# A graph network's update pass with VectorE's sum and shift in the other order, and the root of two norms taken over degree times variance

## The chip, the cores and the metric

One Trainium2 chip (trn2), one of its cores. The kernel is one program with one launch. The metric is the device time of one execution in microseconds (us), taken as the median of repeated runs. TensorE multiplies, VectorE and ScalarE do the elementwise work, GpSimd issues indirect DMAs, and SyncE and ScalarE issue the plain ones.

## The reference, cut to what matters

Four graph layers run over x (10000 nodes by 768 features, fp32), each followed by a layer norm without learned parameters. The parts that the change touches, in the reference's words:

```
x = _layernorm(x + L0(x))          # combined = concat([x, out2]); combined @ Wu + bu     -> update pass
x = _layernorm(x + L1(x))          # relu(heads' residual + attention sum)                -> heads pass
x = _layernorm(x + L2(x))          # graph convolution, norm = dinv[src] * dinv[dst]      -> conv layer "cv"
x = _layernorm(x + L3(x))          # two graph convolutions                               -> "c3a", "c3b"

def _layernorm(x, axis=-1, eps=1e-05):
    m = jnp.mean(x, axis=axis, keepdims=True)
    v = jnp.var(x, axis=axis, keepdims=True)
    return (x - m) / jnp.sqrt(v + eps)
```

A convolution weighs a source row by dinv[src] = 1/sqrt(deg[src]), where deg is the number of edges that end in the node, its own loop among them. The kernel puts that factor into the table that the convolution reads: the heads pass and layer cv write their normed rows times dinv, so the number that they store is (y - m) / sqrt(v + eps) * dinv.

## The kernel before, in words

The 10000 rows are worked in 79 tiles of 128 rows (the last has 16). A stage is a block in which every engine has its own instruction stream over the 79 tiles, written by `over_tiles`: the first four steps are written out, then a loop of four steps a turn, then the last three tiles and the steps that drain the pipeline. The order in each stream is fixed by its `step` function; the engines meet only at semaphores. `back(t, slot, turn, k)` names the tile k steps before the current one; `slot` is the tile's number modulo 4 and `s2` its number modulo 2.

The stages in order of time: first_layers (to about 1276 us of the span), the update pass (`update_pass`, 1280 to 1585 us), the third layer's attention, the heads pass (`heads_pass`, about 1750 to 2095 us), and the conv layers cv, c3a and c3b (`conv_layer`, from about 2100 us to the end).

The update pass, tile t:

- SyncE loads 96 KB of out2 into o2[slot] and 396 KB of u into ut[slot], each once a slot of four is free (for u: once the sum of tile t-4 is made).
- TensorE turns o2 over (`turn_over`, two transposes, in step t), and one step later multiplies it with w_up into one of two PSUM buffers, `prods` (`multiply`, four fp32 products that the trace shows as eight matmul records). The product of tile t waits until the sum of tile t-2 has read its buffer.
- VectorE's `end(t)`: the sum y = prods + ut (L1496), two halves of statistics (L1499, L1500), a memset and their aggregate (L1503), which gives mean and variance in mv.
- ScalarE's `root_of(t)`: root = sqrt(variance + eps) (L1540).
- VectorE's `shift_of(t)`: rstd = 1/root (L1508), shift = -mean*rstd (L1510), and three small pieces of the 25 extra columns (L1511, L1514, L1517). It waits for the root, and for the store of tile t-4, whose x_o buffer it writes.
- ScalarE's `polish(t)`: x_o = y*rstd + shift (L1548), then `store` one step later: 396.5 KB to x1 (L1554) and 12.5 KB to sc3 (L1555).

VectorE's step s runs `shift_of(s-3)` and then `end(s-2)`. ScalarE's step s runs `turn_back(s)` (PSUM to ot, L1535), `root_of(s-2)`, `polish(s-3)` and the store of s-4. `y` has two buffers, so `end(t)` waits until tile t-2 has been polished.

The heads pass and cv end in the same way with their own tiles (hds_, cv_). There `shift_of` has three VectorE instructions: rstd = 1/root (L2148, L2423), rstd = rstd * dinv (L2150, L2426), shift (L2152, L2428). The heads pass also has VectorE's `add` (hds_x, L2128) ahead of these, which TensorE's second six transposes of a tile wait for. In c3b (the last layer) rstd is not multiplied, and c3a has no norm.

Of the kernel before, what the change touches and what calls it, by code (L numbers as in the profile page):

```python
# [8 lines left out]
I32 = mybir.dt.int32  # L9
# [3 lines left out]
P = 128  # L13
N = 10000
E = 12500
D = 768
# [119 lines left out]
def build(nc, a, out):  # L136
# [15 lines left out]
    with ExitStack() as ctx:  # L152
        def sb(name, shape, dt=F32):
# [11 lines left out]
            "one_i": sb("one_i", [P, NT], I32), "sq": sb("sq", [P, NT]),  # L165
# [47 lines left out]
def first_layers(nc, g, a, packed, packed2, sources, agg, h1, sc1, h2, out2, u, x2, x3):  # L213
# [3 lines left out]
    with ExitStack() as ctx:  # L217
# [417 lines left out]
        def _(dve):  # L635
# [137 lines left out]
            bg.to(AT_NODE + 1)  # L773
            dve.wait_ge(deg_root, 1)
# [662 lines left out]
def update_pass(nc, g, u, out2, x1, sc3):  # L1437


    with ExitStack() as ctx:  # L1440
# [6 lines left out]
        y = sb("y", [P, 2, CU])  # L1447
# [39 lines left out]
        def _(dve):  # L1487
            v = nc.vector

            def end(t, slot, turn):  # L1490
                s2 = slot % 2
                dve.wait_ge(u_in[slot], turn * 16 + 16)
                dve.wait_ge(multiplied, t + 1)
                if at_least(t, 2):
                    dve.wait_ge(polished, t - 1)
                v.tensor_tensor(y[:, s2, :].rearrange("p (a f) -> p a f", a=2), prods[s2][:, :, 0:HALFC],  # L1496
                                ut[:, slot, :].rearrange("p (a f) -> p a f", a=2), ALU.add).then_inc(prod_read, 1)
                dve.wait_ge(prod_read, t + 1)
                v.bn_stats(stats[:, s2, 0, :], y[:, s2, 0:HALF]).then_inc(halved, 1)  # L1499
                v.bn_stats(stats[:, s2, 1, :], y[:, s2, HALF:D]).then_inc(halved, 1)  # L1500
                dve.wait_ge(halved, t * 2 + 2)
                v.memset(scrap[:, :], 0.0)
                v.bn_aggr(mv[:, s2, :], stats[:, s2, :, :].rearrange("p a s -> p (a s)")).then_inc(spread, 1)  # L1503

            def shift_of(t, slot, turn):
                s2 = slot % 2
                dve.wait_ge(rooted, t + 1)
                v.reciprocal(rstd[:, s2, :], root[:, s2, :]).then_inc(shifted, 1)  # L1508
                dve.wait_ge(shifted, t * 2 + 1)
                v.scalar_tensor_tensor(shift[:, s2, :], mv[:, s2, 0:1], -1.0, rstd[:, s2, :], ALU.mult, ALU.mult).then_inc(shifted, 1)  # L1510
                v.tensor_scalar(part[:, s2, :], y[:, s2, D:CU], rstd[:, s2, :], None, ALU.mult).then_inc(parted, 1)  # L1511
# [18 lines left out]
        def _(act):  # L1530
# [11 lines left out]
            def polish(t, slot, turn):  # L1542
# [5 lines left out]
                nc.scalar.activation(x_o[:, slot, 0:D], y[:, s2, 0:D], ACT.Identity, bias=shift[:, s2, :],  # L1548
# [482 lines left out]
def heads_pass(nc, g, a, x1, agg, x2):  # L2031
# [4 lines left out]
    with ExitStack() as ctx:  # L2036
# [78 lines left out]
        def _(dve):  # L2115
# [29 lines left out]
            def shift_of(t, slot, turn):  # L2145
# [25 lines left out]
        def _(act):  # L2171
# [6 lines left out]
            def root_of(t, slot, turn):  # L2178
                act.wait_ge(spread, t + 1)
                nc.scalar.activation(root[:, slot % 2, :], mv[:, slot % 2, 1:2], ACT.Sqrt, bias=g["eps"][:, 0:1]).then_inc(rooted, 1)  # L2180

            def polish(t, slot, turn):
                s2 = slot % 2
                act.wait_ge(shifted, t * 3 + 3)
# [60 lines left out]
def conv_layer(nc, g, tag, table, out, weights, bias, res=None, first=False, last=False):  # L2245
# [4 lines left out]
    with ExitStack() as ctx:  # L2250
# [6 lines left out]
        K = 2 if last else 3  # L2257
# [103 lines left out]
        def _(dve):  # L2361
# [58 lines left out]
            def shift_of(t, slot, turn):  # L2420
# [3 lines left out]
                if not last:  # L2424
                    dve.wait_ge(shifted, t * K + 1)
                    v.tensor_scalar(rstd[:, s2, :], rstd[:, s2, :], g["dinv"][:, bass.ds(t, 1)], None, ALU.mult).then_inc(shifted, 1)  # L2426
                dve.wait_ge(shifted, t * K + (K - 1))
# [16 lines left out]
        def _(act):  # L2444
# [32 lines left out]
            def root_of(t, slot, turn):  # L2477
                act.wait_ge(spread, t + 1)
                nc.scalar.activation(root[:, slot % 2, :], mv[:, slot % 2, 1:2], ACT.Sqrt, bias=g["eps"][:, 0:1]).then_inc(rooted, 1)

            def polish(t, slot, turn):
                s2 = slot % 2
                if norm:
                    act.wait_ge(shifted, t * K + K)
# [112 lines left out]
```

## Time and profile before

| What | Value |
|---|---|
| Median of 3 runs | 3884.01 us (3877.66 to 3886.38) |
| The profiled execution's own time | 3883.69 us |
| Its span in the trace | 3881.9 us, 64638 instructions |
| Granted TensorE clock, mean | 0.966 of full |
| TensorE busy, whole span | 3556.3 us (92%) |
| VectorE busy | 2481.6 us (64%) |
| ScalarE busy | 1366.8 us (35%) |
| Update pass, 1300 to 1575 us | TensorE 232.6, VectorE 222.3, ScalarE 120.9 of 275 us |

The page is one execution as the profiler saw it. Busy time is the union of an engine's instructions. The time outside the span is 3883.69 - 3881.9 = 1.8 us. An average over the span says little of one stage, so the stages have to be read one by one: by windows, by the table of waits, and by the timeline of a single tile.

### The profile page before, as it was taken

Reading aid. Unit: us, or ns where it says so; the run is one execution under the profiler, and the core shown is the slowest. Engines: PE = TensorE matmul, PEld = TensorE weight load, DVE = VectorE, ACT = ScalarE, POOL = GpSimd, SP = SyncE. Lnnn points to the kernel's source line nnn. Section 1 sums busy time; section 2 is a strip of 40 time slices with the busy share of each in tenths; the row PEclk is TensorE's granted clock in tenths of the full one; section 3 lists DMA queues with packets and bytes.
Section 4 is the critical chain, followed back from the end, with each engine's and each line's share of the span. In section 5 each row is a group of like instructions: output and inputs, shape, how many; then the busy total and the mean of one; then the engine's idle time right before and its main releaser. Section 6 shows DMA issues by size and latency. Waiting matters only on the chain. (4 is left out here: it accounts for less than half of the span.)

```text
span 3881.9 us, 64638 instructions
## 1 busy us (share of the span) xinstructions
PE 3556.3 (92%) x21125; PEld 3356.1 (86%) x21125; DVE 2481.6 (64%) x4955; ACT 1366.8 (35%) x1888; POOL 1092.4 (28%) x1533
## 2 busy tenths in 40 slices
PE   7999999999999888258996999998899998899999
PEld 6999999999999544138995999997899998799999
DVE  4877986158433588347996777776344443577777
ACT  2222232222222344115664344443333332344443
POOL 5540200414512100427774222221222221322221
PEclk9999999999999999679998999999999999999999
DMA  4777887658754688425665333334333333455554
GB/s 113 238 235 212 238 250 242 190 184 268 225 180 142 198 251 253 139 75 173 212 212 177 104 127 126 126 127 144 108 126 125 127 128 117 157 183 186 184 184 142
DMA packets 363376, 672.37 MB, mean 173 GB/s; under 512 B 100181, under 2 KB 193010, under 8 KB 363242
## 3 DMA queue, kind: packets, MB, share of 16 engines
q1 hardware_dynamic: 248154, 441.01, 37.3%
q10 hardware_dynamic: 70160, 155.79, 10.3%
q0 software_dynamic: 44928, 73.84, 6.8%
q8 instruction: 78, 1.28, 0.1%
q14 instruction: 56, 0.46, 0.0%
HBM read 429.79 MB, written 346.94 MB: 200 GB/s over the span
## 5 line engine op out<-in xcount | busy, mean ns | idle before, releaser
L716 DVE TENSOR_TENSOR fr_lo<-fr_turned_ps,fr_hi 128x768 fp32r<-128x768 f32 x158 | 150.4, 952 | 240.0 <-ACT fr_hi L1140 240.0
L1592 PE MATMUL up_prod<-w_up,up_ot 128*128 128x396 f32 x632 | 231.4, 510 | 40.9 <-DVE up_y L1496 40.9
L2408 DVE SCALAR_TENSOR_TENSOR c3a_y<-c3a_prod,dinv,next_const 128x768 f32<-128x768 f32 x79 | 80.4, 1018 | 288.8 <-PE c3a_prod L2564 288.8
L1284 PE MATMUL fr_prod<-fr_w_hi,fr_hi 128*128 128x396 f32 x948 | 257.1, 352 | 0.0
L1284 PE MATMUL fr_prod<-fr_wu_hi,fr_hi 128*128 128x396 f32 x948 | 254.7, 349 | 0.0
L1284 PE MATMUL fr_prod<-fr_w_lo,fr_hi 128*128 128x396 f32 x948 | 249.3, 344 | 0.0
L2564 PE MATMUL cv_prod<-next_w_hi,cv_hi 128*128 128x384 f32 x948 | 248.9, 344 | 0.0
L2564 PE MATMUL c3a_prod<-next_w_hi,c3a_hi 128*128 128x384 f32 x948 | 248.9, 344 | 0.0
L1284 PE MATMUL fr_prod<-fr_w_hi,fr_lo 128*128 128x396 f32 x948 | 248.7, 343 | 0.0
L2564 PE MATMUL c3b_prod<-next_w_hi,c3b_hi 128*128 128x384 f32 x948 | 248.6, 344 | 0.0
L1284 PE MATMUL fr_prod<-fr_wu_lo,fr_hi 128*128 128x396 f32 x948 | 248.3, 343 | 0.0
L1284 PE MATMUL fr_prod<-fr_wu_hi,fr_lo 128*128 128x396 f32 x948 | 247.8, 342 | 0.0
L2564 PE MATMUL cv_prod<-next_w_hi,cv_lo 128*128 128x384 f32 x948 | 241.8, 336 | 0.0
L2564 PE MATMUL c3a_prod<-next_w_hi,c3a_lo 128*128 128x384 f32 x948 | 241.8, 336 | 0.0
L2564 PE MATMUL cv_prod<-next_w_lo,cv_hi 128*128 128x384 f32 x948 | 241.7, 336 | 0.0
L2564 PE MATMUL c3b_prod<-next_w_lo,c3b_hi 128*128 128x384 f32 x948 | 241.7, 336 | 0.0
L2564 PE MATMUL c3a_prod<-next_w_lo,c3a_hi 128*128 128x384 f32 x948 | 241.6, 336 | 0.0
L2564 PE MATMUL c3b_prod<-next_w_hi,c3b_lo 128*128 128x384 f32 x948 | 241.6, 336 | 0.0
L1140 ACT ACTIVATE fr_hi<-fr_turned_ps 128x768 fp32r<-128x768 f32 x158 | 127.2, 805 | 322.1 <-PE fr_turned_ps L1268 322.0
L1592 PEld LDWEIGHTS up_prod<-w_up,up_ot 128*128 128x128 f32 x632 | 114.7, 191 | 126.0 <-ACT up_ot L1535 44.8
L2475 ACT ACTIVATE c3a_hi<-c3a_turned_ps 128x768 fp32r<-128x768 f32 x79 | 64.1, 812 | 356.2 <-PE c3a_turned_ps L2553 356.2
L2232 PE MATMUL hds_prod<-hds_w_st,hds_hi 128*128 128x128 f32 x948 | 184.3, 276 | 0.0
(588 smaller groups left out, 9109.0 us busy)
## 6 DMA issues: line engine op xcount, KB each, us to landing
fr_ins<-in_x_dram SPq DMA_DIRECT2D x156, 384.0 KB, 4.2
x<-fr_zrow SPq DMA_DIRECT2D x156, 384.0 KB
x<-up_x_o ACTq DMA_DIRECT2D x78, 396.5 KB, 3.5
h<-fr_outs SPq DMA_DIRECT2D x78, 396.0 KB
u<-fr_outs SPq DMA_DIRECT2D x78, 396.0 KB
up_ut<-u SPq DMA_DIRECT2D x78, 396.0 KB
agg<-fr_zrow SPq DMA_DIRECT2D x78, 390.0 KB
hds_row<-x SPq DMA_DIRECT2D x78, 384.0 KB, 3.2
```

The costliest lines, as they stand in the source:

```text
L716: v.tensor_tensor(lo[:, s2, :, :], turned_ps[:, 0:KC, :], hi[:, s2, :, :].bitcast(F32), ALU.subtract).then_inc(split_done, 1)
L1140: nc.scalar.activation(hi[:, t % 2, :, :], turned_ps[:, 0:KC, :], ACT.Copy).then_inc(hi_done, 1)
L1284: made = nc.tensor.matmul(prods[s2][:, bank, 0:c1 - c0], l[:, s2, s, :], w[:, s, c0:c1], start=(s == 0 and i == 0), stop=(s == KC - 1 and ...
L1592: made = nc.tensor.matmul(prods[s2][:, half, 0:HALFC], ot[:, s2, k, :], g["w_up"][:, k, half * HALFC:(half + 1) * HALFC], start=(k == 0), ...
L2232: nc.tensor.matmul(o, hi[:, s2, s, :], w_st[:, 0, :], start=True, stop=False)
L2408: v.scalar_tensor_tensor(y3, p3, g["dinv"][:, bass.ds(t, 1)], c3, ALU.mult, ALU.add).then_inc(prod_read, 1)
L2475: nc.scalar.activation(hi[:, slot % 2, :, :], turned_ps[:, 0:KC, :], ACT.Copy).then_inc(hi_done, 1)
L2564: made = nc.tensor.matmul(prods[s2][:, a, 0:HALF], l[:, s2, s, :], w[:, s, a * HALF:(a + 1) * HALF], start=(s == 0 and i == 0), stop=(s == ...
```

## The change

Three edits.

1. In the update pass, VectorE's step s runs `end(s-2)` first and `shift_of(s-3)` behind it. `y` has four buffers (indexed by slot, not by s2). The wait for the polish moves: `end(t)` no longer waits for `polished`; `shift_of(t)` waits until tile t-1 has been polished.
2. In the heads pass and in cv, the VectorE instruction rstd = rstd*dinv goes. In its place the root is taken of deg*variance + deg*eps: ScalarE's activation reads a column of `deg` as its scale and a column of `deg_eps` as its bias. 1/sqrt(deg*(v + eps)) is the same number as dinv/sqrt(v + eps). c3b keeps its root.
3. In first_layers two VectorE instructions make the two arrays, each 128x79.

The diff, cut to its core:

```
@@ first_layers, after the node lists
+            link(v.tensor_copy(g["deg"][:, :], pt["deg"][:, :]))
+            link(v.tensor_scalar(g["deg_eps"][:, :], pt["deg"][:, :], EPS, None, ALU.mult))
@@ update_pass
-        y = sb("y", [P, 2, CU])
+        y = sb("y", [P, UNROLL, CU])
@@ end(t)
                 dve.wait_ge(multiplied, t + 1)
-                if at_least(t, 2):
-                    dve.wait_ge(polished, t - 1)
-                v.tensor_tensor(y[:, s2, :]..., prods[s2][:, :, 0:HALFC],
+                v.tensor_tensor(y[:, slot, :]..., prods[s2][:, :, 0:HALFC],
...
@@ shift_of(t)
                 dve.wait_ge(rooted, t + 1)
+                if at_least(t, 1):
+                    dve.wait_ge(polished, t)
                 v.reciprocal(rstd[:, s2, :], root[:, s2, :]).then_inc(shifted, 1)
...
@@ step(t)
+                b = back(t, slot, turn, 2)
+                if at_least(t, 2) and live(b[0]):
+                    end(*b)
                 b = back(t, slot, turn, 3)
                 if at_least(t, 3) and live(b[0]):
                     shift_of(*b)
-                b = back(t, slot, turn, 2)
-                if at_least(t, 2) and live(b[0]):
-                    end(*b)
@@ heads_pass and conv_layer (there unless it is the last): shift_of
                 v.reciprocal(rstd[:, s2, :], root[:, s2, :]).then_inc(shifted, 1)
-                dve.wait_ge(shifted, t * 3 + 1)
-                v.tensor_scalar(rstd[:, s2, :], rstd[:, s2, :], g["dinv"][:, bass.ds(t, 1)], None, ALU.mult).then_inc(shifted, 1)
-                dve.wait_ge(shifted, t * 3 + 2)
+                dve.wait_ge(shifted, t * 2 + 1)
@@ root_of
-                nc.scalar.activation(root[...], mv[...], ACT.Sqrt, bias=g["eps"][:, 0:1])
+                nc.scalar.activation(root[...], mv[...], ACT.Sqrt, bias=g["deg_eps"][:, bass.ds(t, 1)],
+                                     scale=g["deg"][:, bass.ds(t, 1)])
```

VectorE's stream at the start of the update pass, before (up_y is the sum, up_mv the aggregate, up_rstd to the second up_x_o the five instructions of the shift; a row is an instruction, with its line, output and inputs):

```order
L1496 TENSOR_TENSOR up_y<-up_prod,up_ut 128x792
L1499 BN_STATS up_stats<-up_y 128x6
L1500 BN_STATS up_stats<-up_y 128x6
L1502 MEMSET up_scrap 128x1
L1503 BN_AGGR up_mv<-up_stats 128x2
L1508 RECIPROCAL up_rstd<-up_root 128x1
L1510 SCALAR_TENSOR_TENSOR up_shift<-up_mv,up_rstd 128x1
L1511 TENSOR_SCALAR up_part<-up_y,up_rstd 128x24
L1514 COPY up_x_o<-own 128x1
L1517 SCALAR_TENSOR_TENSOR up_x_o<-v_sum,up_shift,up_part 128x24
L1496 TENSOR_TENSOR up_y<-up_prod,up_ut 128x792
```

The same place in the changed kernel, from the aggregate of tile 0 on:

```order
L1503 BN_AGGR up_mv<-up_stats 128x2
L1496 TENSOR_TENSOR up_y<-up_prod,up_ut 128x792
L1499 BN_STATS up_stats<-up_y 128x6
L1500 BN_STATS up_stats<-up_y 128x6
L1502 MEMSET up_scrap 128x1
L1503 BN_AGGR up_mv<-up_stats 128x2
L1510 RECIPROCAL up_rstd<-up_root 128x1
L1512 SCALAR_TENSOR_TENSOR up_shift<-up_mv,up_rstd 128x1
L1513 TENSOR_SCALAR up_part<-up_y,up_rstd 128x24
L1516 COPY up_x_o<-own 128x1
L1519 SCALAR_TENSOR_TENSOR up_x_o<-v_sum,up_shift,up_part 128x24
```

The shift of tile 0 stood directly behind the aggregate of tile 0; now the whole sum and statistics of tile 1 stand between them, and so on for every tile: five instructions of a tile's shift are passed by the five of the next tile's sum.

VectorE's stream in one step of the heads pass, before (hds_y is the sum, hds_own_w and hds_x belong to a later tile):

```order
L2122 SCALAR_TENSOR_TENSOR hds_own_w<-hds_more,has_in,has_own 128x12
L2148 RECIPROCAL hds_rstd<-hds_root 128x1
L2150 TENSOR_SCALAR hds_rstd<-hds_rstd,dinv 128x1
L2152 SCALAR_TENSOR_TENSOR hds_shift<-hds_mv,hds_rstd 128x1
L2136 SCALAR_TENSOR_TENSOR hds_y<-hds_prod,hds_row 128x768
```

And in the changed kernel:

```order
L2124 SCALAR_TENSOR_TENSOR hds_own_w<-hds_more,has_in,has_own 128x12
L2150 RECIPROCAL hds_rstd<-hds_root 128x1
L2152 SCALAR_TENSOR_TENSOR hds_shift<-hds_mv,hds_rstd 128x1
L2138 SCALAR_TENSOR_TENSOR hds_y<-hds_prod,hds_row 128x768
```

One instruction has gone between the reciprocal and the shift; nothing else moved. In cv it is the same.

## Rows read from the trace of the kernel before

**Rows 1.** By stretch: length; busy of PE, PEld, DVE, ACT, POOL; clock; DMA share; GB/s.
```profile
1300.00:1575.00 275.00, 232.59 (x744) 127.51 (x742) 222.28 (x750) 120.88 (x224) 0.00 (x0) 1.00 0.83 246
1800.00:2050.00 250.00, 244.13 (x2187) 241.79 (x2186) 228.57 (x608) 161.87 (x183) 198.19 (x243) 1.00 0.65 213
2145.00:2690.00 545.00, 543.20 (x3301) 540.21 (x3299) 426.39 (x859) 226.88 (x307) 102.76 (x220) 1.00 0.36 120
```

**Rows 2.** Waits, update pass: who waited for whom, us, times, longest.
```profile
ACT up_root L1540 <- DVE up_mv L1503: 138.8, 75, 2.2
...
PE up_prod L1592 <- DVE up_y L1496: 40.5, 74, 0.8
DVE up_rstd L1508 <- ACT up_root L1540: 27.2, 75, 0.4
...
DVE up_y L1496 <- ACT up_x_o L1548: 13.6, 58, 0.4
```

**Rows 3.** Timeline, VectorE: start, duration (us), instruction, idle before and its releaser.
```profile
1422.46 0.98 DVE L1496 TENSOR_TENSOR up_y<-up_prod,up_ut 128x792 f32<-128x792 f32 x1 [0.21 <-ACT up_x_o L1548]
...
1424.54 0.20 DVE L1503 BATCH_NORM_AGGREGATE up_mv<-up_stats 128x2 f32<-128x12 f32 x1
...
1425.11 0.16 DVE L1508 RECIPROCAL up_rstd<-up_root 128x1 f32<-128x1 f32 x1 [0.36 <-ACT up_root L1540]
...
1425.65 0.24 DVE L1517 SCALAR_TENSOR_TENSOR up_x_o<-v_sum,up_shift,up_part 128x24 f32<-128x24 f32 x1
1426.09 0.98 DVE L1496 TENSOR_TENSOR up_y<-up_prod,up_ut 128x792 f32<-128x792 f32 x1 [0.20 <-ACT up_x_o L1548]
```

**Rows 4.** The same stretch on ScalarE.
```profile
1424.78 0.29 ACT L1540 ACTIVATE up_root<-up_mv,eps 128x1 f32<-128x1 f32 x1 [1.90 <-DVE up_mv L1503]
1424.98 1.01 ACT L1548 ACTIVATE up_x_o<-up_y,up_shift,up_rstd 128x768 f32<-128x768 f32 x1
```

**Rows 5.** Timeline, TensorE, the first tiles of the update pass.
```profile
1284.50 5.03 PE L1592 MATMUL up_prod<-w_up,up_ot 128*128 128x396 f32 x8
...
1289.59 2.83 PE L1592 MATMUL up_prod<-w_up,up_ot 128*128 128x396 f32 x8
...
1292.47 2.83 PE L1592 MATMUL up_prod<-w_up,up_ot 128*128 128x396 f32 x8
```

**Rows 6.** Timeline, VectorE, tiles 0 and 1 of the update pass.
```profile
1293.85 0.24 DVE L1517 SCALAR_TENSOR_TENSOR up_x_o<-v_sum,up_shift,up_part 128x24 f32<-128x24 f32 x1
1294.01 0.98 DVE L1496 TENSOR_TENSOR up_y<-up_prod,up_ut 128x792 f32<-128x792 f32 x1
```

**Rows 7.** One tile's view, up_y: times, min/median/max ns, first and last start.
```profile
L1496 DVE TENSOR_TENSOR up_y<-up_prod,up_ut x79: 976/983/983, 1289.6 to 1576.4; 128x792 f32<-128x792 f32 x79
```

**Rows 8.** Timeline, ScalarE, last polish of the update pass.
```profile
1579.90 1.03 ACT L1548 ACTIVATE up_x_o<-up_y,up_shift,up_rstd 128x768 f32<-128x768 f32 x1
```

**Rows 9.** DMA issues, update pass: KB each, median us to landing.
```profile
x<-up_x_o ACTq DMA_DIRECT2D x75, 396.5 KB, 3.5
up_ut<-u SPq DMA_DIRECT2D x71, 396.0 KB
up_o<-out SPq DMA_DIRECT2D x70, 96.0 KB, 3.4
```

**Rows 10.** Busy by stretch, the update pass's busiest 5 us for the DMA.
```profile
1540.00:1545.00 5.00, 4.05 (x15) 2.27 (x14) 4.29 (x13) 1.75 (x4) 0.00 (x0) 1.00 0.94 333
```

**Rows 11.** Timeline, VectorE, one tile of the heads pass.
```profile
1900.83 0.16 DVE L2148 RECIPROCAL hds_rstd<-hds_root 128x1 f32<-128x1 f32 x1
...
1901.37 0.16 DVE L2152 SCALAR_TENSOR_TENSOR hds_shift<-hds_mv,hds_rstd 128x1 f32<-128x1 f32 x1
```

**Rows 12.** Waits of TensorE in the heads pass, steady stretch.
```profile
PE hds_turned_ps L2222 <- DVE hds_x L2128: 5.8, 5, 2.1
```

**Rows 13.** Waits of VectorE in the heads pass.
```profile
DVE hds_x L2128 <- issue: 3.5, 12, 0.3
```

**Rows 14.** One line's view, L771: a VectorE operation on 128x79.
```profile
L771 DVE TENSOR_TENSOR fr_node_f<-fr_node_f,fr_node x1: 241/241/241, 244.3 to 244.3; 128x79 f32<-128x79 f32 x1
```

More of the change, by code:

```diff
@@ L164, in build @@
             "total_i": sb("total_i", [P, 1], I32), "total2_i": sb("total2_i", [P, 1], I32),
-            "one_i": sb("one_i", [P, NT], I32), "sq": sb("sq", [P, NT]),
+            "one_i": sb("one_i", [P, NT], I32), "sq": sb("sq", [P, NT]), "deg": sb("deg", [P, NT]), "deg_eps": sb("deg_eps", [P, NT]),
             "src2_i": sb("src2_i", [P, NC], I32), "put2_i": sb("put2_i", [P, NC], I32),
@@ L1547, in polish @@
                     act.wait_ge(stored[slot], turn * 32)
-                nc.scalar.activation(x_o[:, slot, 0:D], y[:, s2, 0:D], ACT.Identity, bias=shift[:, s2, :],
+                nc.scalar.activation(x_o[:, slot, 0:D], y[:, slot, 0:D], ACT.Identity, bias=shift[:, s2, :],
                                      scale=rstd[:, s2, :]).then_inc(polished, 1)
@@ L2179, in root_of @@
                 act.wait_ge(spread, t + 1)
-                nc.scalar.activation(root[:, slot % 2, :], mv[:, slot % 2, 1:2], ACT.Sqrt, bias=g["eps"][:, 0:1]).then_inc(rooted, 1)
+                nc.scalar.activation(root[:, slot % 2, :], mv[:, slot % 2, 1:2], ACT.Sqrt, bias=g["deg_eps"][:, bass.ds(t, 1)],
+                                     scale=g["deg"][:, bass.ds(t, 1)]).then_inc(rooted, 1)
             def polish(t, slot, turn):
                 s2 = slot % 2
-                act.wait_ge(shifted, t * 3 + 3)
+                act.wait_ge(shifted, t * 2 + 2)
                 if at_least(t, UNROLL):
@@ L2256, in conv_layer @@
         L = 2 if apart else 1
-        K = 2 if last else 3
         rows_in = sb("row", [P, UNROLL, D])
@@ L2423, in shift_of @@
                 v.reciprocal(rstd[:, s2, :], root[:, s2, :]).then_inc(shifted, 1)
[L2424 to L2427, printed above, removed]
+                dve.wait_ge(shifted, t * 2 + 1)
                 v.scalar_tensor_tensor(shift[:, s2, :], mv[:, s2, 0:1], -1.0, rstd[:, s2, :], ALU.mult, ALU.mult).then_inc(shifted, 1)
@@ L2478, in root_of @@
                 act.wait_ge(spread, t + 1)
-                nc.scalar.activation(root[:, slot % 2, :], mv[:, slot % 2, 1:2], ACT.Sqrt, bias=g["eps"][:, 0:1]).then_inc(rooted, 1)
+                if last:
+                    nc.scalar.activation(root[:, slot % 2, :], mv[:, slot % 2, 1:2], ACT.Sqrt, bias=g["eps"][:, 0:1]).then_inc(rooted, 1)
+                else:
+                    nc.scalar.activation(root[:, slot % 2, :], mv[:, slot % 2, 1:2], ACT.Sqrt, bias=g["deg_eps"][:, bass.ds(t, 1)],
+                                         scale=g["deg"][:, bass.ds(t, 1)]).then_inc(rooted, 1)
             def polish(t, slot, turn):
@@ L2483, in polish @@
                 if norm:
-                    act.wait_ge(shifted, t * K + K)
+                    act.wait_ge(shifted, t * 2 + 2)
                 else:
```

8 lines of the change are left out of this document (4 added, 4 removed).

## The prediction

> **What bounds the kernel now.** I read the busy shares first, then windows of the stages that the diff touches, then the waits inside them, and last the timeline of single tiles. The page's total (TensorE 92%, in the table above) says that most stages are TensorE's, and the windows say which. In cv TensorE is busy 543.2 of 545 us; in the heads pass 244.1 of 250; in the update pass only 232.6 of 275, with VectorE at 222.3, ScalarE at 120.9 and the DMA engines at 0.83 of full [rows 1]. So the update pass is the one stage of the three in which no engine is full, and a chain through several of them sets the pace. The reader is to look for that chain.
>
> The waits show it: VectorE waits 75 times for the root (27.2 us) and 58 times for the polish (13.6 us), and TensorE waits 74 times for the sum, 40.5 us; ScalarE waits 138.8 us for the aggregate [rows 2]. One tile in order of time: sum at 1422.46, aggregate from 1424.54 to 1424.74 [rows 3], root at 1424.78, polish of the tile before at 1424.98 to 1425.99 [rows 4], next sum at 1426.09 [rows 3]. Every link waits for the one in front, round a ring of 3.63 us. VectorE's shift (1425.11 to 1425.89) lies inside the polish's time. TensorE is in the ring only as a follower: in the first tiles, where no sum had to be waited for, one multiply began 2.88 us after the other (1289.59, 1292.47), with the transposes between them [rows 5]. The first sum starts at 1289.6 and the last at 1576.4, 78 steps of 3.68 us [rows 7].
>
> **The new period of the update pass.** With the sum first, the sum of tile t+1 no longer needs the polish of t-1, as it has a buffer of its own, and the shift of t comes a whole sum and its statistics after the root of t. Both of VectorE's waits in a period, 0.36 and 0.20 us [rows 3], go. 3.63 - 0.36 - 0.20 = 3.07 us. The same from the parts: sum to aggregate 2.08, reciprocal to the last instruction of the shift 1425.65 - 1425.11 = 0.54 [rows 3], and two joints. The joint from the shift's last instruction to a sum that waits for nothing is 0.16 us, less than that instruction's 0.24 [rows 6]; the joint from the aggregate (0.20) to the reciprocal is not in the trace, and taken with the same overlap of 0.08 it is 0.12. Low end: 2.08 + 0.12 + 0.54 + 0.16 = 2.90. High end, each joint a full duration plus 0.04: 2.08 + 0.24 + 0.54 + 0.28 = 3.14. A VectorE that always has work also pays its loop's turn: in the heads pass 0.3 us of "issue" once in four tiles (3.5 us in 12) [rows 13], 0.07 us a tile. So 2.97 to 3.21, and I take 3.05, close to the 3.07 of the subtraction, which is the nearest row.
>
> The Trainium skill, VectorE: DVE Perf Modes, section "The DRAIN you can't avoid", speaks for the high end: an operation does not start before the pipe of the one in front is empty; it adds that one that is not held back starts earlier. By its first sentence the period would be 3.21, by its second the 2.97. The trace has the overlap at the one joint seen (0.08 us) [rows 6].
>
> What is late next? The other cycles are shorter. TensorE: 2.88 us a tile [rows 5]. ScalarE: 120.9 us in 275/3.65 = 75 tiles is 1.61 us [rows 1]. Polish of t-1 now follows the shift of t-1, which follows the aggregate of t; behind the polish ScalarE copies the turned tile for a later multiply, and that feeds a sum three tiles on: about 2.98 (sum to end of shift) + 0.05 + 1.01 (polish) + 0.6 (rest of ScalarE's tile) + 2.83 (multiply) + 0.1 = 7.6 us for three tiles, 2.5 us each. The moved wait stands in front of the reciprocal, with the whole shift and the next sum queued behind it; but the polish of t-2 that it asks for begins when the shift of t-2 ends, some 2.2 us earlier, and takes 1.01. That leaves 1.1 us of cover; without it VectorE, and with it all others, would wait. The root has a full period of cover. SyncE's loads keep their waits and their order; they are asked for earlier, as each sum is.
>
> Sum for the pass. The product of tile 2 is made by 1292.47 + 2.83 = 1295.3 [rows 5]; sum 1 no longer stands behind shift 0, so sum 2 can start then. Sum 78 starts at 1295.3 + 76 x 3.05 = 1527.1, against 1576.4: -49.3 us. The end gets longer. Before, the last polish started 1579.90 - 1576.4 = 3.5 us after the last sum [rows 7, 8]. Now shift 77 stands behind aggregate 78 and ends at 2.98; polish 77 ends at 4.0; only then may shift 78 run (0.78), and polish 78 starts at 4.9: +1.4 us. Together -47.9.
>
> **The other edits.** In the heads pass the removed instruction lies between a reciprocal and a shift that are 0.54 us apart [rows 11]; the reciprocal takes 0.16 of them, so with the instruction gone VectorE gets back up to 0.35 us a tile. TensorE is at 98% there and waited for VectorE's hds_x only 5 times, 5.8 us in 250 [rows 1, 12]. Ends: nothing, if those waits come from late loads, or all of TensorE's idle time, 5.9/250 over some 330 us, 8 us. I take -3, as the next load of a row waits for this tile's sum, which comes earlier. The root with two columns for scale and bias: ScalarE has time to spare (162 of 250 us busy), so 0.1 us more in it costs nothing; if it were on the path it would be 79 x 0.1 = 8 us, kept for the range. In cv TensorE is full to 0.3%: 0, as its products cover VectorE's 0.2 us; uncovered it would be 79 x 0.25 = 20 us of gain, which 543.2 of 545 excludes [rows 1]. First_layers gets two operations on 128x79, 0.24 us each [rows 14] plus a wait: +0.6 us if nothing covers them, 0 if TensorE does; I take +0.3.
>
> Total: 3883.7 (the profiled execution's own time, 0.3 under the median of the runs) - 47.9 - 3 + 0.3 = 3833; with the 0.3 to the median, 3833.4. I say 3834.
>
> **Rivals.** *The DMA becomes the bound.* A tile moves 396.5 + 396 + 96 KB and 12.5 KB more, 901 KB or 0.923 MB [rows 9]; at 3.05 us that is 303 GB/s. For it: 0.83 of full at 246 GB/s puts the ceiling at 296, a period of 3.11 [rows 1]. Against it: 333 GB/s at 0.94 in one stretch of the same pass [rows 10], a ceiling of 354 and 2.6 us. At 3.11 it would cost 5 us and stay in my range. As a rival of its own I take a rate midway between today's and that ceiling, 271 GB/s: 3.40 us, sum 78 at 1553.7, -22.7 + 1.4 - 2.7, so 3860.
>
> On this the Trainium skill, DMA: Bandwidth & Descriptors, section "Where 436 GB/s comes from", gives some 358 GB/s for traffic between HBM and SBUF; by it the period could be 2.6 us, an estimate from that page. The 333 GB/s of rows 10 fits with it.
>
> *VectorE's operations don't overlap:* 3.21 us, sum 78 at 1539.3, -37.1 + 1.4 - 2.7 + 0.3, so 3846. For it stands that only one joint is seen overlapped; against it, that the same engine has no reason to treat the other differently.
>
> *It doesn't do what it says:* a wait of the same size comes back, the moved one for the polish or TensorE's for the copy, and the period stays near 3.6: 3880. Against it are the 1.1 us of cover and the 2.5 us cycle.
>
> *Slower than before: the stores come late.* The shift of t waits until the store of t-4 has landed. That store is issued a step after its shift, so three periods must hold the landing and about 0.7 us: today's 3.5 us [rows 9] needs 1.4 us a tile. From a landing of 10.3 us on the pass is slower than now. Were stores delayed to 12 us by the denser loads, the period would be 4.2 us and the time 3883.7 + 38 + 1 = 3923. Nothing in the trace shows landings near that.
>
> The clock could only hurt: at the half clock of the pass's start a multiply took 5.03 us against 2.83 [rows 5]. TensorE will be busier than in a pass granted 1.00 all along, so I give this nothing.
>
> **How the numbers follow.** Forecast 70%; DMA bound 12%; no overlap 12%; no effect 3%; slower 3%. The forecast's own range is 3822 (2.97 us and all of the heads pass's 8 us) to 3849 (3.21 us, nothing from the heads pass). To leave out no more than 2 in 10 it reaches to the DMA rival: 3821 to 3860. Faster by over 0.2% (8 us, about what a measurement of this kernel can tell from no change): 0.93; within 0.2%: 0.04; slower: 0.03.
>
> **What would show it.** The last sum of the update pass starts near 1527 us, and sums follow at 3.0 to 3.1 us. VectorE's waits for root and polish are gone, and TensorE's for the sum are small or have turned into waits for the copy. VectorE's busy share in the pass passes 90%. DMA at 290 GB/s or more: if instead the share is near 1.0 and VectorE waits for ut, o2 or stores, the DMA rival holds. Reciprocal and shift of the heads pass stand 0.2 us apart, and cv's span is unchanged. I am wrong if sums stay 3.3 us or more apart, or if the gain lies outside the update pass.

## The result, and the profile after

| | before | changed |
|---|---|---|
| Median | 3881.35 us (3877.66 to 3886.38, 4 runs) | 3820.07 us (3816.67 to 3824.79, 4 runs) |
| Profiled execution, its span | 3883.69, 3881.9 us | 3819.96, 3818.0 us |

The ratio is 0.9842 [0.9825, 0.9859], a gain of 61 us. I had said 3834 us with a range from 3821 to 3860. The direction and the place are right, the gain is larger than forecast, and the time lies just under the range. One execution of e1 and one of e2 below fell in a slow state, at 11.2 to 11.3 ms, and both are left out of their times.

First where the 61 us come from. One tile's view of up_y and of hds_y gives the first and last start of each pass's sums (columns: times, min/median/max ns, first and last start). The changed kernel:

```profile
L1496 DVE TENSOR_TENSOR up_y<-up_prod,up_ut x79: 972/977/984, 1287.6 to 1520.9; 128x792 f32<-128x792 f32 x79
...
L2138 DVE SCALAR_TENSOR_TENSOR hds_y<-hds_prod,hds_row x79: 944/958/959, 1711.3 to 2023.2; 128x768 f32<-128x768 f32 x79
```

The kernel before, the sum of the heads pass (its up_y is in [rows 7]):

```profile
L2136 DVE SCALAR_TENSOR_TENSOR hds_y<-hds_prod,hds_row x79: 945/958/959, 1764.7 to 2088.4; 128x768 f32<-128x768 f32 x79
```

The 78 steps of the update pass took 286.8 us (3.68 each) and take 233.3 (2.99). Those of the heads pass took 323.7 (4.15) and take 311.9 (4.00). With the first sum 2.0 us earlier, the update pass's tail 1.5 us longer and some 2 us more spread over the stages between, this is the whole difference of the two spans, 63.9 us. Cv's sums take 537.5 and 537.7 us, as before.

Busy by stretch, changed kernel (length; PE, PEld, DVE, ACT, POOL busy; clock; DMA share; GB/s): update pass, heads pass, cv.

```profile
1300.00:1500.00 200.00, 199.26 (x670) 113.84 (x669) 184.76 (x665) 113.44 (x200) 0.00 (x0) 1.00 0.96 307
1740.00:2000.00 260.00, 260.00 (x2348) 260.00 (x2347) 231.34 (x590) 172.51 (x196) 228.16 (x263) 1.00 0.68 220
2085.00:2630.00 545.00, 539.37 (x3280) 536.40 (x3278) 410.20 (x785) 236.28 (x310) 101.10 (x216) 1.00 0.36 121
```

Against [rows 1], VectorE's share of the update pass went from 81% to 92%, TensorE's from 85% to 99.6%, the DMA's from 0.83 to 0.96, at 307 GB/s. Three things look full at once. Which of them sets the pace can't be read from shares; an experiment below settles it.

Waits in the update pass, changed kernel:

```profile
ACT up_root L1542 <- DVE up_mv L1503: 41.5, 69, 0.8
ACT up_x_o L1550 <- DVE up_x_o L1519: 34.2, 71, 0.6
...
PEld up_prod L1594 <- ACT up_ot L1537: 6.6, 29, 0.3
DVE up_y L1496 <- issue: 6.5, 17, 0.4
```

VectorE's waits for the root and the polish (27.2 and 13.6 us) and TensorE's for the sum (40.5 us) [rows 2] have gone. Only followers wait now. What is left to VectorE is "issue", 17 times, once in four tiles: the turn of its loop. One tile in order of time, changed kernel, VectorE:

```profile
1422.47 0.98 DVE L1496 TENSOR_TENSOR up_y<-up_prod,up_ut 128x792 f32<-128x792 f32 x1
...
1424.55 0.20 DVE L1503 BATCH_NORM_AGGREGATE up_mv<-up_stats 128x2 f32<-128x12 f32 x1
...
1424.67 0.12 DVE L1510 RECIPROCAL up_rstd<-up_root 128x1 f32<-128x1 f32 x1
...
1425.16 0.24 DVE L1519 SCALAR_TENSOR_TENSOR up_x_o<-v_sum,up_shift,up_part 128x24 f32<-128x24 f32 x1
1425.78 0.98 DVE L1496 TENSOR_TENSOR up_y<-up_prod,up_ut 128x792 f32<-128x792 f32 x1 [0.38 <-issue]
```

The two joints that the prediction had to bound are there: aggregate to reciprocal 0.12 us, and shift to sum 0.62 in this step, which holds the turn, 0.16 to 0.20 in the other three of four. The steps in a turn are 2.98, 2.88, 2.85 and 3.31 us, 3.0 on average.

The end of the pass, changed kernel, VectorE:

```profile
1523.60 0.24 DVE L1519 SCALAR_TENSOR_TENSOR up_x_o<-v_sum,up_shift,up_part 128x24 f32<-128x24 f32 x1
1525.06 0.16 DVE L1510 RECIPROCAL up_rstd<-up_root 128x1 f32<-128x1 f32 x1 [1.21 <-ACT up_x_o L1550]
```

Here the moved wait shows for the only time: the last shift stands 1.21 us for the polish of tile 77.

### The profile page after: what moved, and what is told of

Same layout as the page of the kernel before. It is cut to its first block and busy times, and to the rows that moved or that the text cites. A ratio compares the mean times of both kernels' runs of the same rounds, so it can differ in the third digit from the quotient of the medians.

```text
span 3818.0 us, 64399 instructions
## 1 busy us (share of the span) xinstructions
PE 3544.9 (93%) x21125; PEld 3356.4 (88%) x21125; DVE 2428.9 (64%) x4799; ACT 1380.7 (36%) x1888; POOL 1112.7 (29%) x1533
## 5 line engine op out<-in xcount | busy, mean ns | idle before, releaser
L2233 PE MATMUL hds_prod<-hds_w_st,hds_hi 128*128 128x128 f32 x948 | 184.3, 276 | 0.0
L2234 PE MATMUL hds_prod<-hds_w_st,hds_hi 128*128 128x128 f32 x948 | 184.3, 276 | 0.0
```

The costliest lines, as they stand in the source:

```text
L2233: nc.tensor.matmul(o, hi[:, s2, s, :], w_st[:, 0, :], start=True, stop=False)
L2234: made = nc.tensor.matmul(o, hi[:, s2, KC + s, :], w_st[:, 1, :], start=False, stop=True)
```

## The experiments

"Sums" is the time from the first to the last sum of a pass, divided by its 78 steps where "a step" is said; it is read from one profiled execution. "Long shifts" are VectorE's shifts of the heads pass that took over 0.25 us instead of 0.16 in that execution. The ratio is against the kernel before on the same chip.

| Kernel | us | ratio, 95% | update sums | heads sums | long shifts |
|---|---|---|---|---|---|
| before, its profile | 3883.69 | | 286.8 | 323.7 | 8 |
| changed | 3820.07 | 0.9842 [0.9825, 0.9859] | 233.3 | 311.9 | 1 |
| e1 update pass alone | 3827.07 | 0.9867 [0.985, 0.9884] | 235.5 | 319.4 | 5 |
| e2 norms alone | 3873.37 | 0.9989 [0.998, 0.9998] | 286.3 | 312.4 | 1 |
| e3 four buffers, old order | 3931.45 | 1.0139 [1.0124, 1.0153] | 341.2 | 312.1 | 1 |
| e4 new order, two buffers | 3914.14 | 1.0092 [1.0077, 1.0106] | 326.6 | 312.2 | 1 |
| e3b old order, looser wait | 3858.20 | 0.994 [0.9925, 0.9955] | 266.4 | 311.8 | 1 |
| e5 heads pass in the new order | 3872.09 | 0.9977 [0.9968, 0.9986] | 286.6 | 309.9 | 0 |
| e7 rows early in the heads pass | 3944.60 | 1.0168 [1.0153, 1.0184] | | 383.0 | 74 |
| e6 one more instruction there | 3909.94 | one run | | 342.5 | 13 |
| e11 shift of another form | 3877.02 | 0.999 [0.9981, 0.9999] | | 314.7 | 0 |
| e12 changed + e11 + looser wait | 3823.04 | 0.9844 [0.9829, 0.9859] | 233.4 | 311.3 | 0 |
| e9 changed without one copy | 3830.73 | 0.9869 [0.985, 0.9887] | 240.8 | 311.0 | 0 |
| e10b changed, GpSimd busy | 3838.06 | one run | 251.0 | 312.2 | 1 |
| e13 changed, half the products | 3818.04 | one run | 234.3 | 312.6 | 1 |
| e14 before once more | 3877.23 | one run | 286.6 | 315.1 | 2 |

**e1 and e2: the two halves of the change.** e1 is the kernel before with the changed `update_pass`; e2 is the changed kernel with the old one.

> The kernel before with only the update pass changed (order, four buffers, moved wait); the two norms keep their multiplication by dinv. Theory: the update pass gives some 52 us of the 61 measured, and the heads pass keeps its 328 us, since its own instructions are untouched: time about 3829 to 3832, last sum of the update pass near 1521 to 1523 us. Rival (the heads pass gains from something that the update pass hands on, such as where tiles lie in memory or when it starts): the heads pass falls to some 316 us here too, and the time is about 3820.

> The kernel before with only the root over the degree, and the two arrays that it needs. Theory: the heads pass falls by 10 to 12 us from 328 (first sum to last polish), cv and the update pass stay: about -0.3%, 3869 to 3872. Rival (the 12 us belong to the update pass's change): within 0.1% of before. Rival of the record (heads -3 us): 3878.

The update pass alone gives -51.5 us (7 either way), as expected. The norms alone give -4 (-8 to -1): not the -0.3% that e2 was expected to give, but about the -3 of the prediction. Together that is 56, within the change's own interval of 55 to 68. The heads pass's share of 11.8 us in the two profiles is thus not what that edit is worth. Before's sums there took 323.7 us in one profiled execution and 315.1 in another (e14), with 8 and 2 long shifts.

**e3, e4, e3b: order and buffers apart.** e3 is the changed kernel with VectorE's step in its old order:

```
             def step(t, slot, turn):
+                b = back(t, slot, turn, 3)
+                if at_least(t, 3) and live(b[0]):
+                    shift_of(*b)
                 b = back(t, slot, turn, 2)
                 if at_least(t, 2) and live(b[0]):
                     end(*b)
-                b = back(t, slot, turn, 3)
-                if at_least(t, 3) and live(b[0]):
-                    shift_of(*b)
```

> The changed kernel with VectorE's old order in the update pass (shift of tile t, then sum of t+1), but with four buffers for y and the sum free of the polish. Theory: the wait for the polish (0.20 us) goes and the wait for the root (0.36) stays: a period of 3.45 us instead of 2.99, so some 35 us slower than the changed kernel, 3853 to 3858. Rival (the buffers alone were the lock, the order brings nothing): within 3 us of the changed kernel.

e4 is e2 (the update pass of before) with the step in the new order and nothing else of the pass changed, so `y` keeps two buffers and `end(t)` its wait for the polish of t-2.

> The changed kernel with the new order but two buffers for y, and the wait for the polish in front of the sum as before. Theory: the polish of t-1 now starts when the shift of t-1 ends, directly ahead of the sum of t+1, which waits for all of it: period 2.85 + 1.1 = 3.95 to 4.05 us, the pass 75 to 80 us longer than with four buffers, so 3895 to 3900, slower than before. Rival (the order alone does it, the polish is quick enough): within 5 us of the changed kernel.

Each alone makes the pass slower than it was. e3 was a plain miss, 4.37 us a step against the expected 3.45; e4 went the expected way and further, 4.19 against 3.95 to 4.05. e3, VectorE: one tile.

```profile
1422.07 0.20 DVE L1503 BATCH_NORM_AGGREGATE up_mv<-up_stats 128x2 f32<-128x12 f32 x1
...
1423.67 0.16 DVE L1510 RECIPROCAL up_rstd<-up_root 128x1 f32<-128x1 f32 x1 [1.40 <-ACT up_x_o L1550]
```

I had overlooked that the wait "shift of t after the polish of t-1" was moved with the buffers. In the old order that polish starts only behind the root of t in ScalarE's stream, so the ring is aggregate, root, polish, shift, sum: 4.37 us a step. e4, VectorE:

```profile
1425.41 0.24 DVE L1519 SCALAR_TENSOR_TENSOR up_x_o<-v_sum,up_shift,up_part 128x24 f32<-128x24 f32 x1
1426.87 0.98 DVE L1498 TENSOR_TENSOR up_y<-up_prod,up_ut 128x792 f32<-128x792 f32 x1 [1.22 <-ACT up_x_o L1550]
```

With two buffers the sum of t waits for the polish of t-2, which in the new order begins only when the shift just before that sum has ended: 4.19 us a step. e3b is e3 with the wait that is really needed for the buffers of rstd and shift:

```
-                if at_least(t, 1):
-                    dve.wait_ge(polished, t)
+                if at_least(t, 2):
+                    dve.wait_ge(polished, t - 1)
```

> The changed kernel with VectorE's old order, four buffers, the sum free of the polish, and a looser wait in front of the reciprocal: the shift of t waits for the polish of t-2, whose rstd it overwrites, not for that of t-1. Theory (two locks, the polish and the root, each worth its own wait): only the root's wait stays in the ring, sum to sum 3.35 us plus the loop's turn, 3.42 on average, so the pass's 79 sums take some 267 us against 286.8 before and 233.3 in the changed kernel: near 3852. Rival (the moved wait was harmless in the run before this one and something else made 4.37 us): still above 4 us a tile, over 3900.

It came out at 3.415 us a step against the expected 3.42. One tile, VectorE:

```profile
1425.00 0.20 DVE L1503 BATCH_NORM_AGGREGATE up_mv<-up_stats 128x2 f32<-128x12 f32 x1
...
1425.56 0.16 DVE L1510 RECIPROCAL up_rstd<-up_root 128x1 f32<-128x1 f32 x1 [0.36 <-ACT up_root L1542]
```

The wait for the polish is gone, that for the root (0.36 us, as in [rows 3]) is not. So four buffers are worth 20 us of sums (286.8 to 266.4) and the order, which takes the root off the path, another 33 (266.4 to 233.3), but only on top of the buffers.

**e13: who sets the pace now.** The changed kernel with half of the products of the update pass left out (the k = 1 half of each is not multiplied, so its output is not the reference's):

```
-                    for k in range(2):
-                        made = nc.tensor.matmul(..., start=(k == 0), stop=(k == 1))
+                    for k in range(1):
+                        made = nc.tensor.matmul(..., start=True, stop=True)
```

> The changed kernel with half of TensorE's products of the update pass left out (each half of the row takes one of the two products, so out2's second part and the constant are missing). TensorE's work per tile falls from 2.88 to some 1.56 us. Theory (VectorE sets the pace: 2.86 us and the loop's turn): sum to sum stays at 2.86 to 3.0 with 3.3 once in four, all sums 228 to 233 us. Rival (TensorE, or the copy in front of it, sets the pace): the steps of 2.98 shrink to 2.86 and the turn's 3.31 too, sums below 226 us.

```profile
1300.00:1500.00 200.00, 129.25 (x401) 59.66 (x399) 184.81 (x663) 113.75 (x200) 0.00 (x0) 1.00 0.96 307
```

TensorE's busy time fell from 199.26 to 129.25 us, and the sums kept their step (3.004 against 2.991). VectorE sets the pace; TensorE's 99.6% was that of a follower that fits closely (2.88 of 2.99 us). DMA moves 307 GB/s in both, and VectorE's only waits in the steady part of the changed pass are the 17 of its loop, none for a load or a store. Whether DMA would go faster is not shown here.

**e9: an instruction less on the engine that is full.** The changed kernel without the copy of the own column (L1516, 0.15 us), whose column of x_o is set to zero once at the start:

```
+            v.memset(x_o[:, :, D + 24:D + 25], 0.0).then_inc(col_zero, 1)
...
-                v.tensor_copy(x_o[:, slot, D + 24:D + 25], g["own"][:, bass.ds(t, 1)]).then_inc(scored, 1)
```

> The changed kernel, with VectorE's copy of the own column (L1516, 0.13 us a tile) left out of the update pass: the column is zero in what is stored. Theory (VectorE sets the pace there, 2.86 us and 0.46 for the loop's turn once in four tiles; TensorE needs 2.88): the period falls from 2.99 to 2.88 to 2.90, the sums from 233 to 225 to 227 us. Rival (TensorE or the copy that feeds it sets the pace): 233 us as before.

It got slower, against both the theory and the rival: 3.09 us a step instead of 2.99. One tile, VectorE of e9:

```profile
1421.34 0.23 DVE L1515 TENSOR_SCALAR up_part<-up_y,up_rstd 128x24 f32<-128x24 f32 x1
1421.78 0.24 DVE L1520 SCALAR_TENSOR_TENSOR up_x_o<-v_sum,up_shift,up_part 128x24 f32<-128x24 f32 x1 [0.21 <-DVE up_part L1515]
```

The last instruction of the shift reads what L1515 writes. In the changed kernel the copy stands between them and the two start 0.27 us apart (0.37 once in four tiles); without it VectorE waits for its own result and they start 0.32 apart (0.44 once in four). The copy had filled a wait. The mean distance grew from 0.29 to 0.35 us, 0.06 of the 0.10 us a step; the rest is spread over the other joints and is not explained.

**e5, e6, e7, e11, e14: what the heads pass gained from.** At first two theories stood: that VectorE's work in a step counts (0.35 us less a tile), and that single steps are disturbed, by rows that come late or by what depends on them, as the prediction had it. A third came from the traces of these runs: that the shift itself is held now and then. e5 is before with the heads pass in the update pass's new form: four `y`, the sum ahead of the shift, rstd\*dinv kept.

```
-        ... y = sb("y", [P, 2, D])
+        ... y = sb("y", [P, UNROLL, D])
                 dve.wait_ge(rooted, t + 1)
+                if at_least(t, 1):
+                    dve.wait_ge(polished, t)
```

> The kernel before with the heads pass alone changed: sum ahead of the shift, four buffers for y, multiplication by dinv kept. VectorE's work per tile stays the same, but each sum, and with it the next load of a row, comes earlier. Theory A (work: VectorE's own 3.98 us a tile is as long as TensorE's 3.99, so nothing is caught up after a late row; only less work on VectorE helps): the heads pass stays at 319 to 324 us for its sums, the time within 0.1% of before. Theory B (load: a row asked for earlier is never late): its sums take 312 us, the time falls by 4 to 12 us.

With the instruction kept, the sums took 309.9 us, less than the changed kernel's 311.9, and there was no long shift: less work is not what the pass gained from. The number is the one of theory B, but e5 moves the shift as well as the loads, so it can't tell the second theory from the third. e7 is before with the residual left out of the heads pass's sum (a fixed array of zeros stands for it), so that rows can be loaded two steps earlier; e6 is before with a second, unused product of rstd and dinv in each shift.

```
-                    sp.wait_ge(prod_read, t - UNROLL + 1)
+                    sp.wait_ge(turned, t - UNROLL + 1)
...
-                                       row[:, slot, :].rearrange("p (a f) -> p a f", a=2), ALU.max, ALU.add)
+                                       fixed[:, :].rearrange("p (a f) -> p a f", a=2), ALU.max, ALU.add)
```

> The kernel before, but the heads pass leaves out the residual: its sum adds a tile of zeros and not the row, so that a row's buffer is free when TensorE has turned it over, two steps earlier than the sum. VectorE's work per tile is the same. Theory A (work): GpSimd's waits for hds_row go, but the steady pace is VectorE's 3.98 us; with no late row there is nothing to catch up either, so the sums take 312 us if late rows are the only disturbance, and stay above 317 if VectorE's fullness loses time by itself. Theory B (load): 312 us, and no wait for hds_row over 0.5 us.

```
+                v.tensor_scalar(junk[:, s2, :], rstd[:, s2, :], g["dinv"][:, bass.ds(t, 1)], None, ALU.mult).then_inc(shifted, 1)
```

> The kernel before with one more instruction of the kind that the change removes in the heads pass: rstd*dinv a second time into a tile that nobody reads, with its own wait. If VectorE stands at the edge (theory A), it now sets the pace alone: 3.98 + 0.25 to 0.35 = 4.25 to 4.35 us a tile, sums in 332 to 340 us, the time 10 to 18 us longer. If VectorE had slack in the pass (rival), the sums stay at 319 to 324 us.

e6 took 342.5 us, a little over what was expected, with 13 long shifts. Between them four of its steps take 4.10, 4.10, 4.10 and 4.59 us, 0.24 a step more than in before, as theory A had it; the held shifts make the rest. In before the steps between the long ones are 3.86, 3.86, 3.85 and 4.34 us, 3.98 on average, and the changed kernel's average 3.99. The steady pace did not change, so the 11.8 us lie at the long shifts, where nine steps of before take 4.8 to 6.4 us.

e7 went against both theories: nearly every shift became long. In before GpSimd's product hds_x waited 34 times for a row (25.6 us); in e7 it never did, waited mostly for VectorE, and came to start some 0.3 us ahead of the shift. One tile of e7, VectorE and GpSimd:

```profile
1901.34 1.47 POOL L2101 TENSOR_TENSOR hds_x<-hds_row,hds_own_w 128x768 f32<-128x768 f32 x1 [1.41 <-DVE hds_x L2130]
1901.40 0.21 DVE L2152 TENSOR_SCALAR hds_rstd<-hds_rstd,dinv 128x1 f32<-128x1 f32 x1
1901.65 1.17 DVE L2154 SCALAR_TENSOR_TENSOR hds_shift<-hds_mv,hds_rstd 128x1 f32<-128x1 f32 x1
```

One of the eight of the kernel before:

```profile
1854.03 2.21 DVE L2152 SCALAR_TENSOR_TENSOR hds_shift<-hds_mv,hds_rstd 128x1 f32<-128x1 f32 x1
1854.73 1.49 POOL L2099 TENSOR_TENSOR hds_x<-hds_row,hds_own_w 128x768 f32<-128x768 f32 x1
```

Both shifts end within 0.02 us of the end of GpSimd's product (1901.34 + 1.47 = 1902.81 against 1902.82; 1856.22 against 1856.24). The tensor_scalar that runs inside the product, at 1901.40, takes its usual 0.21. Over the whole pass of e7, 75 shifts start inside a product and 74 of them are held (the other started 0.04 us before the product's end); 55 tensor_scalars start inside one and none takes over 0.22. In all runs every long shift ends 0.01 to 0.03 us after a product. So the shift is held by GpSimd's product, and the form of the instruction matters. e11 tests that: before with the same shift written so that rstd comes in as a column scalar and one tensor is read instead of two.

```
-                v.scalar_tensor_tensor(shift[:, s2, :], mv[:, s2, 0:1], -1.0, rstd[:, s2, :], ALU.mult, ALU.mult)
+                v.tensor_scalar(shift[:, s2, :], mv[:, s2, 0:1], rstd[:, s2, :], -1.0, ALU.mult, ALU.mult)
```

> The kernel before with one edit in the heads pass: the shift (L2152) is a tensor_scalar, which reads mv as its only tensor and rstd as a column scalar, and not a scalar_tensor_tensor, which reads both as tensors. As many instructions, and the multiplication by dinv stays. Theory (collision): the pass loses its 8 to 12 us where the shift falls into GpSimd's product hds_x and is held until that ends, as 2.21 us instead of 0.16 in the trace of before; a shift with one tensor is not held, so it never takes over 0.3 us, the sums take 312 to 314 us, and the time falls by 4 to 11 us. Rival (late rows): the shift's form is indifferent, sums stay at 319 to 324 us, and pairs of steps of 5.5 to 6.4 us stay.

The shift in e11, min/median/max:

```profile
L2152 DVE TENSOR_SCALAR hds_shift<-hds_mv,hds_rstd x79: 213/214/216, 1768.1 to 2080.9; 128x1 f32<-128x1 f32 x79
```

The same in the kernel before:

```profile
L2152 DVE SCALAR_TENSOR_TENSOR hds_shift<-hds_mv,hds_rstd x79: 159/160/2215, 1769.5 to 2091.4; 128x1 f32<-128x1 f32 x79
```

No shift is held, though two start inside a product, and the pass takes 314.7 us, just over the expected 312 to 314, as each shift now takes 0.05 us more. The time fell by 4 us (0.4 to 7), as in e2. GpSimd still waited 40 times for a row (18.5 us), and in the changed kernel 41 times (16.6): late rows stayed and cost nothing that can be seen.

The Trainium skill, SBUF — State Buffer, section "Who interferes with whom", says what fits with this: a VectorE instruction with two inputs in SBUF contends with a GpSimd instruction that reads SBUF, and is blocked, not slowed, until that one is done, while one with a single SBUF input isn't (outside the modes that use both ports). By it the start decides who is held; in the second fence above the shift starts 0.7 us ahead of the product, with an indirect DMA of GpSimd ending between, so either the record of GpSimd's start is rough or something else of GpSimd's held it. That stays open.

One input alone does not keep a VectorE instruction free of every GpSimd instruction. At the start of before's update pass GpSimd clears an array:

```profile
1280.47 13.32 POOL L1470 MEMSET rows_x<- 128x15860 f32 x1
...
1292.49 0.16 DVE L1510 SCALAR_TENSOR_TENSOR up_shift<-up_mv,up_rstd 128x1 f32<-128x1 f32 x1
1292.57 1.25 DVE L1511 TENSOR_SCALAR up_part<-up_y,up_rstd 128x24 f32<-128x24 f32 x1
```

Inside the memset, which reads nothing, the shift with its two tensors takes its usual 0.16 us, and the tensor_scalar of 128x24, usually 0.23, ends 0.03 us after the memset. It did so in all ten runs in which it started inside this memset (0.85 to 1.55 us). What holds what thus depends on both instructions.

> The kernel before once more, unchanged, for a second trace of its heads pass. Theory (a shift that falls into GpSimd's product is chance): again single steps of 5.4 to 6.4 us between steps of 3.86 and 4.35, with shifts of over 1 us at them, in another number and at other tiles, so the sums take 316 to 324 us. Rival (fixed places): 323.7 us, at the same tiles as in the first trace.

The kernel before again: two long shifts, at other tiles (1887.01, 2068.28) than the eight of the first profile, and 315.1 us, a little under the expected 316. The three profiles with the heads pass of before (before, e14, e1) had 8, 2 and 5 long shifts; the eight with the instruction gone and nothing else new in the pass (changed, e2, e3, e4, e3b, e9, e10b, e13) had none or one, and that one always at the first tile of the pass, where the shift still falls into a product. The instruction's removal starts the shift sooner: from its start to the next product's start the median is 1.04 us in the changed kernel and 0.59 in before.

**e10b: the collision made on purpose.** The changed kernel with 40 products of 128x768 on GpSimd (on arrays of its own) in the update pass, one after each of the sums of tiles 9 to 48:

```
+            for i in range(40):
+                pool.wait_ge(prod_read, 10 + i)
+                nc.gpsimd.tensor_tensor(busy[:, 2, :], busy[:, 0, :], busy[:, 1, :], ALU.mult).then_inc(busy_done, 1)
...
```

> The changed kernel; in the update pass GpSimd also multiplies two tiles of 128x768 into a third that nobody reads, once after each of 40 sums (tiles 9 to 48), about 1.5 us each. It measures the collision by itself, in a pass where GpSimd otherwise does nothing after its first 13 us. Theory (collision): GpSimd starts at a sum's end, where the statistics run; instructions of VectorE with two tensors in SBUF that fall into it are held until it ends, those with one are not. The shift (L1512) and L1519 are the ones with two; they come 1.2 us after the sum, so some are held up to 0.5 us, and steps there are longer by as much. Rival: no VectorE instruction changes its duration.

```profile
1340.85 1.80 POOL L1478 TENSOR_TENSOR up_busy<-up_busy 128x768 f32<-128x768 f32 x1 [1.52 <-DVE up_y L1503]
...
1341.93 0.12 DVE L1517 RECIPROCAL up_rstd<-up_root 128x1 f32<-128x1 f32 x1
...
1342.08 0.60 DVE L1519 SCALAR_TENSOR_TENSOR up_shift<-up_mv,up_rstd 128x1 f32<-128x1 f32 x1
1342.60 0.23 DVE L1520 TENSOR_SCALAR up_part<-up_y,up_rstd 128x24 f32<-128x24 f32 x1
```

The shift ends at 1342.68 and the product at 1342.65. The reciprocal inside the product takes its usual 0.12. All forty shifts are held, and forty holds of 0.44 us are 17.6 us; the pass's sums grew by 17.7. That also says once more that VectorE is the bound.

**e12: both findings on top of the change.** The changed kernel with e3b's looser wait and e11's shift.

> The changed kernel with two more edits: the shift of the heads pass in the form with one tensor, and in the update pass the shift of t waits for the polish of t-2, not of t-1. Theory: the update pass's last polish starts 3.9 us after its last sum instead of 5.0 (shift 78 need not wait for polish 77), and nothing else in the pass changes; the heads pass loses its one remaining step of 5.9 us. Together 1 to 3 us less than the changed kernel. Rival: the looser wait also shortens each period (the polish of t-1 was late at times): over 5 us less.

The tail went from 5.0 to 4.0 us (3.9 expected), the sums of neither pass moved by over 0.6 us, and 0.9844 against 0.9842 is no difference that this measurement can tell: the expected 1 to 3 us are neither shown nor excluded. The change already had one long shift only, so there was nothing left to take.

## Why the prediction came out low in its gain

What held, in the order of the prediction:

- The ring and its breaking: VectorE's two waits of a period went, TensorE's for the sum with them, and e13 shows VectorE as the bound. The period taken from the subtraction was 3.05 us; it is 2.99. The two joints came out at the low end (0.12 and 0.16 us), the loop's turn at 0.46 us in four tiles instead of 0.3: 2.85 + 0.12 = 2.97 to 3.0, near the stated low end of 2.97. Of the two sentences taken from the Trainium skill, VectorE: DVE Perf Modes, section "The DRAIN you can't avoid", the second is the one that holds here, at both joints: the reciprocal starts 0.12 us after an aggregate that takes 0.20, the sum 0.16 after an instruction of 0.24.
- The pass's term: -49.3 foreseen, -53.5 measured, of which 76 steps by 0.06 us are 4.6. The tail: +1.4 foreseen, +1.5 measured. Together -47.9 against -52.0, and -51.5 by e1 alone.
- The cover of the moved wait: no such wait in the steady pass, only at the end. e3 shows what it costs where the cover is missing, 1.4 us a tile.
- DMA: 303 GB/s foreseen, 307 measured at a share of 0.96, without becoming the bound. The rivals "DMA", "no overlap", "no effect" and "slower" are all refuted by the 2.99 us a step; the ceiling that 0.83 at 246 GB/s seemed to set, 296, was passed.
- The root with two columns takes longer, 0.377 us in the heads pass and 0.387 in cv (medians) against 0.295, near the 0.1 us more that was allowed for. ScalarE had room for it: cv's sums take 537.7 us against 537.5.

The step that failed is the heads pass's: "Ends: nothing, ... or all of TensorE's idle time, 5.9/250 over some 330 us, 8 us. I take -3". In the two profiles the pass got 11.8 us shorter, over the bound. The 64 us between the profiles are -52.0 (update pass), -11.8, -2.0 (the first sum's start, which scatters from 1287 to 1296 us over all kernels and is chance) and +2 elsewhere. The heads pass gave 8.8 us more than forecast and the update pass 4.1; the time lies 0.9 us under the range, and without either excess it would have been inside.

Three errors lie in the heads pass's term. The first is its mechanism. The gain does not come from an earlier load of a row; it comes from shifts that are no longer held behind GpSimd's product (e11, e7, e10b), and the row of the spread was there to be read: min/median/max 159/160/2215 ns for a 128x1 instruction. I read one tile's shift alone [rows 11]. The second is the bound: it took one stretch of 250 us for the whole pass, and only four of the eight held shifts lie in that stretch; in it TensorE's busy time was itself a little stretched (244.13 us for 2187 instructions, 0.1116 each, against 0.1107 after). The third is the start of the sum: 3883.7 us is the time of an execution with eight held shifts, and the same kernel took 3877.23 in one with two (e14). Against that execution the heads pass gained 3.2 us, and by e2 the edit is worth -4 [-8, -1] against the median of before. That the -3 is near these is luck, as it was reached by a mechanism that is not at work.

The forecast's own sum came to 3833.4, which rounds to 3833 and not to 3834.

First_layers: the two added operations cost nothing that can be seen. The first sum of the update pass starts at 1287.1 (e2, with them) and 1288.3 (e1, without), and between 1287 and 1296 over all kernels.

What stays open: e1 and e2 add up to 56 us and the change measured 61; their intervals cover the difference, and no run tells whether the 5 us are real.

## What to carry to other kernels

Where waits form a ring, change the order, the buffers and the wait that guards them together: here the new order with the old buffers made the kernel 0.9% slower, the new buffers in the old order with the moved wait 1.4% slower and with a looser wait 0.6% faster, and all together gave 1.3%. Ask of every moved wait which instruction of the other engine it needs and what stands ahead of that one in its stream. Read the maximum of tiny instructions beside their median, since a column operation that takes 0.16 us as a rule and 2.2 us at times is being held by somebody; and before removing an instruction from a full engine, look whether it fills a wait of the next.

## What the runs showed of the hardware

- A VectorE instruction that reads two SBUF tensors (scalar_tensor_tensor, 128x1) and starts inside GpSimd's 128x768 product ends with it: 0.16 us became 0.60 (e10b, 40 of 40) and 1.17 (e7, 74 of 75). One that started 0.7 us ahead of the product ended with it too, after 2.21 us (before). The same arithmetic as tensor_scalar with a column scalar took 0.213 to 0.216 us in all 79 tiles of e11, two of them inside a product.
- Beside a memset of GpSimd it was the other way round: the two-tensor 128x1 instruction took 0.16 us, and a tensor_scalar of 128x24 was held until the memset's end, 1.25 us instead of 0.23 (before).
- The turn of a loop costs VectorE 0.46 us in its own stream once in four tiles, even where it is the bound: 0.62 us instead of 0.16 from the shift's last instruction to the next sum.
- Independent small VectorE instructions start about 0.07 to 0.15 us apart while each takes 0.15 to 0.24, but a dependent pair in e9 started 0.32 to 0.44 apart.
- A square root of 128x1 on ScalarE took 0.295 us with one column (the bias) and 0.377 to 0.387 with two (scale and bias).
- The DMA engines held 307 GB/s of mixed loads and stores for 200 us at a share of 0.96.
